# Routing weights of the expert layers spread by DMA from DRAM instead of by TensorE

## The chip, the cores and the metric

The program runs on one core of a Trainium2 chip. The metric is the time of one execution on the device in microseconds (us), the median of several.

## The reference

Tokens are 2 x 1024 vectors of 128 elements. Eight blocks follow one another, each a residual x + f(x), mostly of a layer norm: window attention, a Fourier layer, global and local attention, the Fourier layer again, a location attention, a mixture of experts, a relu-attention block with a feed-forward, and the mixture of experts once more with the same weights. The change is in the mixture of experts, which runs twice:

```python
scores = jax.nn.sigmoid(xt @ gate_w.T)
_, idx = lax.top_k(scores + gate_b, 4)                    # of 16 experts
w = jnp.take_along_axis(scores, idx, axis=-1)
w = w / jnp.sum(w, axis=-1, keepdims=True) * 2.5
comb = zeros((T, 16)).at[arange(T)[:, None], idx].add(w)  # 0 where an expert is not chosen
for each expert e:
    y = y + comb[:, e][:, None] * ((silu(xt @ w1[e].T) * (xt @ w3[e].T)) @ w2[e].T)
y = y + (silu(xt @ w1_s.T) * (xt @ w3_s.T)) @ w2_s.T      # shared expert
```

All 16 experts are computed for every token, and comb puts to zero what wasn't chosen. An expert has 64 hidden rows.

## The kernel before

Activations lie with the 128 features on the partitions and the 2048 tokens along the free axis, in four chunks (c) of 512. Experts are taken in eight pairs (j): a pair fills the 128 partitions with 64 hidden rows of each. Everything of weights and constants stays in SBUF; the engines are programmed by hand, each with its own instruction order, and meet by semaphores. `bank(n)` is one of eight PSUM banks of 128x512 fp32. An fp32 matmul makes two records in the profile. All of TensorE's matmuls carry line 1572, that of the helper `mm`.

`moe_layer` stands once for each engine (lines 685, 971, 1387 and 1917), and is called twice, with i = 0 and 1. Its stages:

- **Logits**: 16 matmuls a half on TensorE give 16 scores a token, tokens on partitions. ACT takes the exponential (line 973), and DVE works out the routing weights `cw` in some ten steps (lines 1407 to 1436), each waiting for the one before (`m_d`). Four more steps (1442 to 1448) split `cw` into three bf16 parts, `cparts`, whose sum is the fp32 value.
- **Early loop** (`ahead`, line 1927): while DVE routes, TensorE makes gate and up of the shared expert (a = 0, 1) and of all eight pairs of chunk 0 (a = 2 to 9); ACT takes silu of gate and copies up (lines 981, 982), POOL multiplies the two (line 695) into buffers from which `hidden_of(a)` reads.
- **Spreading**: TensorE transposes `cparts` by 16 bf16 products with the identity into banks 4 to 7, ACT copies these to `comb` (line 986), 96 rows of bf16 with the three parts stacked. For each (c, j) `spread` (line 1955) multiplies `comb` by a 0/1 matrix from the bf16 constants `bsb`: in PSUM each of a pair's 64 rows per expert then holds that expert's weight for the 512 tokens.
- **Pairs** (line 1979): in the order of (c, j) TensorE issues gate and up of the next pair (not for chunk 0, which has them), the spread of the next pair, the shared expert's down product where j = 0, and the down product of this pair, which accumulates in bank 4 + c. ACT takes silu (line 994) when `m_gu` says that the pair's spread, and so all ahead of it, is done. DVE multiplies up by silu (line 1466), and that by the spread weights in PSUM (line 1469; line 1462 for chunk 0), into `moe[:, 2, k % 2]`, of which there are two; `m_h` releases the down product. At j = 1 DVE adds the chunk before to the residual x (line 1105).

Before the layer POOL clears `cparts` and part of `comb` (lines 688, 690). SyncE issues all DMAs; in the expert layers it has nothing to do but to wait for the output chunks, whose stores are the last four.

## Time and profile before

| | us |
|---|---|
| median of 3 runs | 1099.7 (1099.45 to 1100.71) |
| the profiled execution | 1103.62 |
| its span | 1101.6 |
| TensorE (PE) busy in it | 999.0 (91%) |
| VectorE (DVE) busy | 572.7 (52%) |
| ScalarE (ACT) busy | 557.3 (51%) |
| GpSimd (POOL) busy | 154.3 (14%) |
| mean granted clock of TensorE | 0.936 |

The span is the time from the first to the last instruction in the profile; what the execution takes above it lies around the program. PEld is the loading of weights, which overlaps the products; a busy TensorE is not one at its peak. The chain of work that ended last is followed back from the last instruction, at each step to what released it. A row's bracket tells how long the engine had been idle before it, and what ended that.

### The profile page before, as it was taken

What the parts mean: (1) busy time and instruction counts of PE and PEld (TensorE: products, weight loads), DVE (VectorE), ACT (ScalarE), POOL (GpSimd) and SP (SyncE); (2) the same over time, 40 slices, a digit from 0 to 9 for tenths busy, and PEclk for the clock granted to TensorE, in tenths of its full rate; (3) what the DMA queues carried; (4) which work ended last, traced back from release to release, by engine and by line L of the source; (5) the groups of instructions that cost most, each with busy time, mean ns of one, the idle gap of its engine ahead of it and who ended that gap; (6) DMA issues with size and microseconds to landing.
All of it is one profiled execution on the core that took longest, in us unless ns stands there. A gap on an engine that the chain in (4) does not pass through costs nothing.

```text
span 1101.6 us, 22066 instructions
## 1 busy us (share of the span) xinstructions
PE 999.0 (91%) x9528; PEld 460.5 (42%) x9528; DVE 572.7 (52%) x1134; ACT 557.3 (51%) x767; POOL 154.3 (14%) x168
## 2 busy tenths in 40 slices
PE   6578988989999999877989799998999999999998
PEld 3345655343333334665433344433333333353443
DVE  4465672562333446556455554545666665425454
ACT  5114445659999965543655551127454555445111
POOL 3300102022100101111001140000123223104000
PEclk9569999999999999677999889999999999998999
DMA  9653301000000000000000000000000000000000
GB/s 303 161 142 92 88 17 41 0 20 21 2 3 2 2 2 0 4 4 2 1 0 1 0 1 0 1 0 1 1 3 2 2 3 2 0 1 1 10 10 19
DMA packets 8312, 26.49 MB, mean 24 GB/s; under 512 B 3148, under 2 KB 3468, under 8 KB 6668
## 3 DMA queue, kind: packets, MB, share of 16 engines
q1 hardware_dynamic: 8216, 25.09, 8.3%
q8 instruction: 75, 1.23, 0.5%
q14 instruction: 21, 0.17, 0.1%
HBM read 20.56 MB, written 4.29 MB: 23 GB/s over the span
## 4 chain that ended last, share of the span: by engine, by line
PE 77%; DVE 8%; ACT 8%; issue 3%; DMA 2%; POOL 0%; SPq 0%; DVEq 0%; POOLq 0%
PE ps L1572 76%; ACT nrr L778 1%; ACT nrr L776 1%; DMA stf<-aux 1%; DVE masked L1174 1%; DVE mxq L1180 1%; ACT work L1025 1%; DMA stf<-scr_k 1%; DVE work L1134 1%; DVE work L1526 0%; ACT nrr L765 0%; ACT nrr L762 0%; DVE stf L1540 0%; ACT work L1019 0%; ACT stf L986 0%
## 5 line engine op out<-in xcount | busy, mean ns | idle before, releaser
L1572 PE MATMUL ps<-rq,stf 32*64 32x512 f32 (+4 forms) x4096 | 204.9, 456 | 5.0 <-ACT hz L929 1.6
L1572 PE MATMUL ps<-work,vbuf 64*32 64x96 f32 (+8 forms) x3200 | 202.3, 402 | 6.8 <-issue 5.7
L1572 PE MATMUL ps<-hz,wsb 128*128 128x512 f32 (+1 forms) x352 | 161.1, 623 | 4.0 <-ACT nsq L767 3.5
L885 ACT ACTIVATE work<-ps 128x1024 f32<-128x1024 f32 x144 | 139.4, 1023 | 13.2 <-PE ps L1572 8.9
L1572 PEld LDWEIGHTS ps<-rq,stf 32*64 32x64 f32 x4096 | 95.4, 144 | 107.7 <-issue 79.5
L1572 PEld LDWEIGHTS ps<-work,vbuf 128*32 128x32 f32 (+1 forms) x3200 | 72.7, 119 | 122.4 <-issue 70.1
L947 ACT ACTIVATE work<-ps 128x1024 f32<-128x1024 f32 x72 | 73.7, 1025 | 75.6 <-PE ps L1572 75.6
L824 ACT ACTIVATE work<-ps 128x768 f32<-128x768 f32 x64 | 51.5, 812 | 99.4 <-PE ps L1572 99.4
L1572 PEld LDWEIGHTS ps<-hz,wsb 128*128 128x128 f32 (+1 forms) x352 | 62.9, 191 | 87.7 <-issue 71.2
L994 ACT ACTIVATE work<-ps 128x512 f32<-128x512 f32 x48 | 28.7, 597 | 134.5 <-PE ps L1572 134.5
L1572 PE MATMUL ps<-work,wsb 128*128 128x512 f32 (+1 forms) x176 | 92.6, 622 | 2.7 <-DVE work L1469 2.7
L1247 DVE TENSOR_TENSOR work<-work,csb 128x1024 f32<-128x1024 f32 (+1 forms) x40 | 40.7, 1017 | 96.0 <-ACT work L885 95.6
L1572 PE MATMUL ps<-bsb 128*128 128x384 bf16 x192 | 67.3, 352 | 21.7 <-DMA stf<-scr_k 7.2
L1309 DVE TENSOR_SCALAR work<-ps 128x1024 f32<-128x1024 f32 (+3 forms) x72 | 68.5, 953 | 24.2 <-PE ps L1572 24.2
L1466 DVE TENSOR_TENSOR work<-ps,work 128x512 f32<-128x512 f32 x48 | 33.2, 692 | 72.5 <-ACT work L994 70.8
L1180 DVE TENSOR_REDUCE mxq<-ps 128x2 f32<-128x384 f32 x64 | 35.6, 556 | 44.5 <-PE ps L1572 43.4
L753 ACT ACTIVATE nsq<-ps 128x512 f32<-128x512 f32 x40 | 23.9, 597 | 61.3 <-PE ps L1572 61.3
L682 POOL TENSOR_TENSOR work<-work,csb 128x512 f32<-128x512 f32 (+1 forms) x40 | 36.4, 910 | 106.7 <-ACT work L947 106.7
L1572 PEld LDWEIGHTS ps<-work,wsb 128*128 128x128 f32 (+1 forms) x176 | 31.9, 193 | 44.6 <-issue 20.9
L1572 PE MATMUL ps<-nsq,csb 128*128 128x512 f32 (+3 forms) x152 | 45.0, 516 | 5.1 <-DVE nrr L1263 1.9
L663 POOL TENSOR_SCALAR aux<-nsq,csb 128x1024 f32<-128x1024 f32 x8 | 22.8, 2844 | 159.0 <-DVE nsq L1234 109.2
L1572 PE MATMUL ps<-stf 88*128 88x192 bf16 (+1 forms) x256 | 44.3, 277 | 0.4
(203 smaller groups left out, 1292.1 us busy)
## 6 DMA issues: line engine op xcount, KB each, us to landing
wsb<-in_w SPq DMA_DIRECT2D x1, 3440.0 KB, 19.9
stf<-scr_k SPq DMA_DIRECT2D x12, 204.0 KB
stf<-scr_q SPq DMA_DIRECT2D x12, 192.0 KB
csb<-in_c SPq DMA_DIRECT2D x1, 2099.0 KB, 9.8
rq<-in_rq SPq DMA_DIRECT2D x2, 1024.0 KB, 5.2
scr_q<-work SPq DMA_DIRECT2D x6, 256.0 KB, 6.6
scr_k<-work SPq DMA_DIRECT2D x6, 256.0 KB, 6.3
rq<-scr_k SPq DMA_DIRECT2D x6, 204.0 KB
```

The lines of the kernel that those rows point to most:

```text
L663: nc.gpsimd.tensor_scalar(nums[:, b * S:(b + 1) * S], half_out[0][:, b * S:(b + 1) * S], c_("part")[:, 0:1], None, ALU.mult).then_inc(q["s ...
L682: nc.gpsimd.tensor_tensor(cells, cells, c_("keep").unsqueeze(1).unsqueeze(1) .broadcast_to(list(cells.shape)), ALU.mult).then_inc(q["mk"], 1)
L753: nc.scalar.activation(nsq[:, c], bank(c), ACT.Square).then_inc(n_sq, 1)
L824: nc.scalar.activation(dst, src, ACT.Exp, scale=SCALE).then_inc(q["ex"], 1)
L885: nc.scalar.activation(probs_of(n)[:, 2 * k:2 * k + 2].rearrange("p h s -> p (h s)"), two(slot(2 * n + k)), ACT.Exp, scale=SCALE).then_inc ...
L947: nc.scalar.activation(probs_of(n)[:, 0:2].rearrange("p h s -> p (h s)"), two(slot(2 * n)), ACT.Relu, scale=SCALE).then_inc(q["ex"], 1)
L994: nc.scalar.activation(moe[:, 0, k % 2], bank(k % 2), ACT.Silu).then_inc(m_sg, 1)
L1180: nc.vector.tensor_reduce(mxq[:, k % 2, 2 * u:2 * u + 2], bank(4 + m % 2)[:, 0:2 * W_A].rearrange("p (t s) -> p t s", t=2), AX.X, ALU.max) ...
L1247: nc.vector.tensor_tensor(cells, cells, c_("keep").unsqueeze(1).unsqueeze(1) .broadcast_to(list(cells.shape)), ALU.mult).then_inc(q["mk"], 1)
L1309: ins = nc.vector.tensor_scalar(to[:, :, lo:hi], src[:, :, lo:hi], SCALE, 0.0, ALU.mult, ALU.max)
L1466: nc.vector.tensor_tensor(moe[:, 1, k % 2], bank(2 + k % 2), moe[:, 0, k % 2], ALU.mult)\
L1572: return nc.tensor.matmul(o, l, r, start=start, stop=stop, skip_group_check=True)
```

## The change

The routing weights stay fp32. TensorE transposes `cw` itself (`route_rows`, 16 fp32 transposes, one group of four after each of the early products a = 5 to 8, the first behind a wait for `cw`), ACT copies the 16 rows to `cwt` in SBUF between its early operations, and SyncE stores each chunk of 16x512 to a DRAM tensor `scr_w`. From there SyncE loads for each (c, j) two transfers, one for each expert: 64 partitions, each with the same row of 512 fp32. They go to a ring of eight buffers, `share`, in SBUF; the load of pair k waits till pair k - 8 has been multiplied (`m_h`). DVE's second multiply reads the share from SBUF instead of the spread weights from PSUM, after a wait for the two DMAs (`m_w`). Removed are the spreads, the splitting into three parts, POOL's two memsets, and the matrix of 1024 columns in the bf16 constants. `m_gu` is raised by the up product, `ROUTE_STEPS` is 12.

```diff
+SHARES = 8
-BCOLS = [("ident", 128), ("band_q", 2 * W_A), ("band_a", 2 * W_A),
-         ("spread", NPAIR * 128)]
+BCOLS = [("ident", 128), ("band_q", 2 * W_A), ("band_a", 2 * W_A)]
...
-        comb = stf[:, 0:T // 2].bitcast(BF16)
+        cwt = stf[0:NE, 0:T]
+        share = stf[:, 2 * T:2 * T + SHARES * CH].rearrange("p (k s) -> p k s", k=SHARES)
...
+        scr_w = nc.dram_tensor("scr_w", (NE, T), F32, kind="Internal").ap()
...
+            def shares(i):
+
+                def store(c):
+                    sp.wait_ge(m_cs, NC * i + c + 1)
+                    sp.dma_start(scr_w[:, c * CH:(c + 1) * CH], cwt[:, c * CH:(c + 1) * CH]).then_inc(m_st[c], 16)
+
+                def load(c, j):
+                    k = (i * NC + c) * NPAIR + j
+                    if k >= SHARES:
+                        sp.wait_ge(m_h, k - SHARES + 1)
+                    for e in range(2):
+                        sp.dma_start(share[HB * e:HB * (e + 1), k % SHARES],
+                                     scr_w[2 * j + e, c * CH:(c + 1) * CH].unsqueeze(0).broadcast_to([HB, CH]))\
+                            .then_inc(m_w[k % SHARES], 16)
+
+                store(0)
+                sp.wait_ge(m_st[0], 16 * (i + 1))
+                for j in range(NPAIR):
+                    load(0, j)
+                for c in range(1, NC):
+                    store(c)
+                for c in range(1, NC):
+                    sp.wait_ge(m_st[c], 16 * (i + 1))
+                    for j in range(NPAIR):
+                        load(c, j)
...
             rope_load(1)
+            shares(0)
+            shares(1)
             for c in range(NC):
                 sp.wait_ge(s_res, 4 * U_M1 + c + 1)
...
-                nc.gpsimd.memset(cparts, 0.0).then_inc(m_z, 1)
-                nc.gpsimd.memset(comb[96:P, :], 0.0).then_inc(m_z, 1)
...
+                def rows(c):
+                    act.wait_ge(m_t, NC * i + c + 1)
+                    nc.scalar.activation(cwt[:, c * CH:(c + 1) * CH], bank(4 + c)[0:NE], ACT.Copy).then_inc(m_cs, 1)
...
                     nc.scalar.activation(moe[:, 4, a % 2], bank(2 + a % 2), ACT.Copy).then_inc(e_a, 1)
-                for c in range(NC):
-                    act.wait_ge(m_t, NC * i + c + 1)
-                    nc.scalar.activation(comb[0:96, c * CH:(c + 1) * CH], bank(4 + c)[0:96], ACT.Copy)\
-                        .then_inc(m_cs, 1)
+                    if ROUTED < a <= ROUTED + NC:
+                        rows(a - ROUTED - 1)
...
-                done(nc.vector.tensor_copy(cparts[:, :, 0, 0:NE], cw))
-                done(nc.vector.tensor_tensor(rest, cw, cparts[:, :, 0, 0:NE], ALU.subtract))
-                done(nc.vector.tensor_copy(cparts[:, :, 1, 0:NE], rest))
-                done(nc.vector.tensor_tensor(cparts[:, :, 2, 0:NE], rest, cparts[:, :, 1, 0:NE], ALU.subtract))
...
                         if c == 0:
                             dve.wait_ge(e_m, AHEAD * i + 3 + j)
-                            dve.wait_ge(m_gu, k + 1)
-                            nc.vector.tensor_tensor(moe[:, 2, k % 2], bank(spread_bank(c, j)), hidden_of(2 + j),
+                            dve.wait_ge(m_w[k % SHARES], 32 * (k // SHARES + 1))
+                            nc.vector.tensor_tensor(moe[:, 2, k % 2], hidden_of(2 + j), share[:, k % SHARES],
                                                     ALU.mult).then_inc(m_h, 1)
                             continue
...
                         dve.wait_ge(m_su, full(i, c, j) + 1)
-                        nc.vector.tensor_tensor(moe[:, 2, k % 2], bank(spread_bank(c, j)), moe[:, 1, k % 2],
+                        dve.wait_ge(m_w[k % SHARES], 32 * (k // SHARES + 1))
+                        nc.vector.tensor_tensor(moe[:, 2, k % 2], moe[:, 1, k % 2], share[:, k % SHARES],
                                                 ALU.mult).then_inc(m_h, 1)
...
-                    mm(bank(2 + k % 2), w_("w_up")[:, j * P:(j + 1) * P], ch(z, c))
-                def spread(c, j):
-                    mm(bank(spread_bank(c, j)), b_("spread")[:, j * P:(j + 1) * P], ch(comb, c)).then_inc(m_gu, 1)
+                    mm(bank(2 + k % 2), w_("w_up")[:, j * P:(j + 1) * P], ch(z, c)).then_inc(m_gu, 1)
+                def route_rows(c):
+                    pe.wait_ge(m_d, ROUTE_STEPS * (i + 1))
+                    for tt in range(4):
+                        ins = nc.tensor.transpose(bank(4 + c)[0:NE, tt * P:(tt + 1) * P],
+                                                  rt[:, (4 * c + tt) * NE:(4 * c + tt + 1) * NE], c_("ident"))
+                    ins.then_inc(m_t, 1)
...
                 for a in range(AHEAD):
                     ahead(a)
-                pe.wait_ge(m_d, ROUTE_STEPS * (i + 1))
-                for c in range(NC):
-                    for tt in range(4):
-                        ins = mm(bank(4 + c)[0:96, tt * P:(tt + 1) * P],
-                                 cparts[:, 4 * c + tt].rearrange("p i e -> p (i e)"), b_("ident"))
-                    ins.then_inc(m_t, 1)
-                pe.wait_ge(m_cs, NC * (i + 1))
-                spread(0, 0)
+                    if ROUTED <= a < ROUTED + NC:
+                        route_rows(a - ROUTED)
                 todo = [(c, j) for c in range(NC) for j in range(NPAIR)]
                 for n_, (c, j) in enumerate(todo):
                     if n_ + 1 < len(todo):
                         if todo[n_ + 1][0]:
                             gate_up(*todo[n_ + 1])
-                        spread(*todo[n_ + 1])
                     if j == 0:
+                        pe.wait_ge(m_cs, NC * i + c + 1)
                         shared_down(c)
```

## Rows read from the trace of the kernel before

**Rows 1.** The page, shares of the chain that ended last, by engine

```profile
PE 77%; DVE 8%; ACT 8%; issue 3%; DMA 2%; POOL 0%; SPq 0%; DVEq 0%; POOLq 0%
```

**Rows 2.** Timeline, pair of chunk 1, layer one (start us, length us, engine, line)

```profile
684.67 1.02 PE L1572 MATMUL ps<-work,wsb 128*128 128x512 f32 x2
...
684.87 0.60 ACT L994 ACTIVATE work<-ps 128x512 f32<-128x512 f32 x1 [2.19 <-PE ps L1572]
...
685.53 1.88 PE L1572 MATMUL ps<-hz,wsb 128*128 128x512 f32 x4
...
686.30 0.69 DVE L1469 TENSOR_TENSOR work<-ps,work 128x512 f32<-128x512 f32 x1
...
687.46 1.02 PE L1572 MATMUL ps<-work,wsb 128*128 128x512 f32 x2
```

**Rows 3.** Timeline, from the early loop to chunk 1, first layer

```profile
646.43 0.67 DVE L1436 SCALAR_TENSOR_TENSOR stf<-stf 128x256 f32<-128x256 f32 x1
...
648.95 0.19 PEld L1572 LDWEIGHTS ps<-hz,wsb 128*128 128x128 f32 x1 [0.29 <-ACT work L982]
...
656.20 1.06 PE L1572 MATMUL ps<-bsb,stf 128*96 128x128 bf16 x16
...
659.48 0.60 PE L1572 MATMUL ps<-stf,bsb 128*128 128x512 bf16 x2 [2.22 <-ACT stf L986]
...
670.33 1.88 PE L1572 MATMUL ps<-hz,wsb 128*128 128x512 f32 x4
```

**Rows 4.** Stretches, handover of both layers (engines busy, granted clock, DMA share, GB/s)

```profile
656.20:670.33 14.13, 11.91 (x42) 4.80 (x41) 5.31 (x8) 3.02 (x6) 2.18 (x2) 0.88 0.00 0
...
1010.96:1025.08 14.12, 11.90 (x41) 4.80 (x40) 5.31 (x8) 3.02 (x6) 2.17 (x2) 0.88 0.01 1
```

**Rows 5.** Timeline, last pair of the first layer

```profile
741.86 0.69 DVE L1469 TENSOR_TENSOR work<-ps,work 128x512 f32<-128x512 f32 x1
...
742.60 1.13 PE L1572 MATMUL ps<-work,wsb 128*128 128x512 f32 x2 [1.35 <-DVE work L1469]
```

**Rows 6.** Timeline, an addition with two operands in SBUF

```profile
973.37 0.69 DVE L1114 TENSOR_TENSOR x<-x,hz 128x512 f32<-128x512 f32 x1
```

**Rows 7.** Timeline, transposes ahead of the location attention

```profile
542.61 0.60 PE L2035 MATMUL ps<-csb,hz 128*128 128x128 f32 x4
...
543.04 1.02 PE L1572 MATMUL ps<-hz,wsb 128*128 128x512 f32 x2
```

**Rows 8.** Timeline, start of chunk 1 of the first layer

```profile
674.83 0.38 PE L1572 MATMUL ps<-stf,bsb 128*128 128x512 bf16 x1
...
678.87 0.38 PE L1572 MATMUL ps<-stf,bsb 128*128 128x512 bf16 x1
```

**Rows 9.** DMA issues (KB, median us to landing); issue durations ns, min/median/max

```profile
csb<-in_c SPq DMA_DIRECT2D x1, 128.0 KB, 2.1
...
out_x<-x SPq DMA_DIRECT2D x4, 256.0 KB, 2.0
...
L532 SPq DMA_DIRECT2D stf<-scr_q x12: 651/692/793, 32.1 to 103.8; - x12
...
L538 SPq DMA_DIRECT2D stf<-scr_k x12: 314/366/551, 38.2 to 105.7; - x12
```

**Rows 10.** Timeline, DVE and POOL side by side during the first layer's early loop

```profile
645.23 0.43 DVE L1429 TENSOR_TENSOR stf<-stf 128x256 f32<-128x256 f32 x1
...
648.98 1.30 POOL L695 TENSOR_TENSOR aux<-work 128x512 f32<-128x512 f32 x1 [0.43 <-ACT work L982]
...
649.19 1.37 DVE L1448 TENSOR_TENSOR stf<-stf 128x256 bf16<-128x256 f32 x1
```

**Rows 11.** Stretches, two with loads from the DRAM scratch tensors

```profile
38.20:47.00 8.80, 1.65 (x8) 1.35 (x7) 1.08 (x5) 0.00 (x0) 0.06 (x1) 0.50 0.56 95
...
83.00:95.00 12.00, 8.96 (x86) 5.95 (x85) 5.37 (x26) 3.96 (x5) 0.65 (x2) 0.86 0.52 118
```

**Rows 12.** DMA issues, the bf16 constants

```profile
bsb<-in_b SPq DMA_DIRECT2D x1, 480.0 KB, 5.4
```

More of the change, by code:

```diff
@@ L271, in build @@
         m_t = sem("route_transposed")
-        m_z = sem("route_room_zeroed")
-        m_cs = sem("route_stack")
+        m_st = [sem(f"route_stored{c}") for c in range(NC)]
+        m_w = [sem(f"share_loaded{n}") for n in range(SHARES)]
+        m_cs = sem("route_rows")
         s_ws = sem("shared_down_weights_copied")
@@ L432, in build @@
         AHEAD = 2 + NPAIR
-        ROUTE_STEPS = 16
+        ROUTE_STEPS = 12
+        ROUTED = 5
         SETS = [
@@ L990, in moe_layer @@
                         k = (i * NC + c) * NPAIR + j
-                        act.wait_ge(m_gu, k + 1)
+                        act.wait_ge(m_gu, full(i, c, j) + 1)
                         if full(i, c, j) >= 2:
@@ L1434, in moe_layer @@
                 after()
-                dve.wait_ge(m_z, 2 * (i + 1))
                 done(nc.vector.scalar_tensor_tensor(out=cw, in0=w8, scalar=ROUTE,
@@ L1438, in moe_layer @@
                                                     op0=ALU.mult, op1=ALU.mult))
-                rest = s_
-                after()
-                done(nc.vector.tensor_copy(cparts[:, :, 0, 0:NE], cw))
-                after()
-                done(nc.vector.tensor_tensor(rest, cw, cparts[:, :, 0, 0:NE], ALU.subtract))
-                after()
-                done(nc.vector.tensor_copy(cparts[:, :, 1, 0:NE], rest))
-                after()
-                done(nc.vector.tensor_tensor(cparts[:, :, 2, 0:NE], rest, cparts[:, :, 1, 0:NE], ALU.subtract))
                 assert step[0] == k0 + ROUTE_STEPS
@@ L2165, in bfloat_constants @@
     put("band_a", np.tile(np.where(ok, 0.0, NEG), (1, 2)))
-    spread = np.zeros((P, NPAIR, 2, INTER), np.float32)
-    for e in range(NE):
-        for part in range(3):
-            spread[32 * part + e, e // 2, e % 2, :] = 1.0
-    put("spread", spread.reshape(P, -1))
     return c.astype(BF16_NP)
```

9 lines of the change are left out of this document (removed).

## The prediction

> **What bounds the kernel now.** I read the chain that ended last first: TensorE holds 77% of it, so what leaves TensorE's queue in a stretch where nothing else is late leaves the time too [rows 1]. Then I read the timelines of the two expert layers, because the change touches nothing else but one load at the start. Each layer has three stretches.
>
> In the main one (chunks 1 to 3, 24 expert pairs) the order on TensorE is gate and up of the next pair (four records of 0.43 us), spread of the next pair, down of this one (two records). One pair takes 2.79 us from down to down (684.67 to 687.46). The two records of a down take 0.86, until gate and up start at 685.53 [rows 2]. Six fp32 records at 0.43 fill 2.58, the spread the 0.21 that are left: TensorE is full. Beside it runs a chain of latency: silu starts 0.20 us after the spread has streamed (684.67 to 684.87), then come 0.60 of ACT and two DVE multiplies, the last of which ends at 686.99 [rows 2], in time for the down at 687.46, but not by much.
>
> The stretch ahead of it is the handover: when the last early gate and up product is done TensorE transposes the routing parts (from 656.20), waits 2.22 us for the four ACT copies, starts spreading at 659.48, and reaches gate and up of chunk 1 at 670.33 [rows 3]. That is 14.1 us, and the same stretch of the second layer takes 14.1 us too (1010.96 to 1025.08) [rows 4]. Of useful work only one shared product and seven down products lie in it. The granted clock over it is 0.88 in both layers [rows 4]: TensorE sits idle inside it, and part of it then runs at 1.2 GHz in place of 2.4. In the new order it has no such gap, so I cost chunk 0 at 2.4 GHz.
>
> The third stretch is the early loop: gate and up for two shared and eight routed pairs, four records or 1.72 us each. Its routing weights are ready early: cw starts at 646.43 and takes 0.67, so it is there at 647.10, while the weights of the seventh early pair (a = 6) load at 648.95 [rows 3].
>
> **The change, part by part.**
>
> *Spreads removed, chunks 1 to 3.* 24 a layer at 0.215 us (2.79 less six records of 0.43 [rows 2]): 5.2 us a layer. The signal to ACT moves from the spread to the up product, so the latency chain starts 0.21 earlier too. Counted from the end of the up product it will be as long as it is now from the end of the spread, 684.67 to 686.99 = 2.32 us. Then 0.05 to the weight load (742.55 to 742.60 at the layer's last pair [rows 5]) and at most 0.19 for that load [rows 3]: 2.56. TensorE meanwhile has a down and a gate and up = 2.58. Margin 0.02 us, or more where the load is quicker. DVE gets a further wait (for the share) ahead of its second multiply, and behind it on DVE are only the next pair's multiplies and the chunk's residual; I take it at nothing and bound it by the margin being overrun by 0.05 us a pair, 1.2 us a layer (below nothing it can't go: TensorE has no less to do). The multiply itself now reads two SBUF operands: 0.69 us, as the residual's SBUF add of the same shape shows [rows 6], against 0.69 from PSUM [rows 2]. No gain and no loss there.
>
> *Handover.* New order: after early pair 5, and again after 6, 7 and 8, four fp32 transposes of 128x16. The 128-column transposes of the location attention stand four in 0.43 us (542.61 to 543.04) [rows 7]; 16 cost 1.72 us a layer. They need the routing weights at 648.95 and find them 1.85 us old, so the new wait of TensorE there ends at once. The four copies go between ACT's early work: 1.19 + 0.60 us of ACT beside 2.15 of TensorE, hidden. The early loop ends at 656.20 + 1.72 = 657.9. The shared product of chunk 0 comes at once; such a product adds 4.04 - 2.79 = 1.25 us where it stands in chunk 1 (674.83 to 678.87) [rows 8]. So down of pair 0 may start at 659.2.
>
> Its share must be there: the copy of row block 0 follows early pair 6 (its products end at about 651.5, ACT adds 0.2 + 1.1 + 0.6), 653.4. Store issued at 653.5. A 256 KB store of 2 KB rows lands 2.0 us after its issue, a 128 KB load from DRAM 2.1 [rows 9]. Store landed 655.5, loads from 655.6, the second load of the pair 0.45 later, landed 658.1. Multiply and latency 0.95: 659.1. So the round trip through DRAM is just hidden. After it pairs come at the slowest of three rates: TensorE 0.86, the double-buffered hidden tile 0.96 (from the end of one down: 0.2 to DVE, 0.69, 0.05 and some 0.1 back, 0.86 of the down after next, for two pairs), and the loads. SyncE takes 0.37 us to issue a plain load and 0.69 for one whose source repeats rows [rows 9]; a pair has two, so 0.75 to 1.4 us. I take 1.0, nearest to the plain ones, since this source has only two dimensions. Seven pairs then bring gate and up of chunk 1 to 665.9, against 670.33: 4.4 us. At 0.86 a pair it would be 5.1, at 1.4 a pair 2.1.
>
> *A lock between DVE and POOL.* Two DVE operations on 128x256 with two SBUF inputs take 0.43 and 1.37 us; the long one started at 649.19 beside a POOL product that ran from 648.98 to 650.28, and ended 0.28 after it [rows 10]. The spread multiplies read PSUM; the new ones read two SBUF operands, and POOL's last early product (which shifts with the loop to about 659.4 to 660.7) lies just beside the first ones. At worst one multiply waits 1.3 us for it. I take off half, 0.6 us a layer. The Trainium skill (SBUF — State Buffer, SBUF: two separate sides) says the same in general: DVE with two SBUF inputs and a POOL operation that reads SBUF exclude each other for a whole instruction. By that rule every one of the 32 multiplies is of the kind that can be blocked; by the trace only those beside POOL's last product would be.
>
> *DMA volume.* 64 loads of 128 KB a layer. The final store lands 256 KB of 2 KB rows in 2.0 us with all its fixed parts [rows 9]: a load is at most 1.0 us of the DMA engines, 64 us a layer of some 85, and less as they overlap. Each load is issued up to eight pairs (20 us) ahead. The Trainium skill (SBUF — State Buffer, Door 1) speaks against this shape: 64 partitions reach only eight of the sixteen ports, some 196 GB/s, and two transfers to the two halves serialize. By that, as an estimate, a load takes 0.65 us, a pair 1.3; the handover would gain some 2.5 us in place of 4.4, and the main stretch would gain as much as before; that is within the first rival below. No row here shows 64 partitions loaded alone.
>
> *Nothing for:* POOL's two memsets, DVE's four splitting steps (the last, the long one above, ended at 650.56, TensorE took them up at 656.20 [rows 3, 10]), the stores of chunks 1 to 3 (SyncE issues them behind the first 16 loads, at about 663, lands them at 665; chunk 1 needs its first share at about 669), the output stores queued behind the last loads. If the issue of the first 16 loads took 1.4 a pair, this cover goes and chunk 1 waits about 1 us.
>
> *Start.* The bf16 constants lose 1024 columns, 256 KB of 480 [rows 12]. Other loads share the engines then, and the first stretch also waits on POOL and ACT, so it may bring nothing; at most it brings what 256 KB cost beyond the fixed part, about half of the 2.0 us above [rows 9]. Between 0 and 1 us; I take 0.5.
>
> **Sum.** (5.2 + 4.4 - 0.6) x 2 + 0.5 = 18.5 us. The profiled execution took 1103.62 with a span of 1101.6; it would take 1085.1. The median of the runs, 1099.7, lies 3.9 lower, and the same saving gives 1081.2; I say 1081.
>
> **The rivals.**
>
> *Loads set the pace of chunk 0.* At 0.69 an issue, 6.3 us a layer remain (2.1 - 1.0 + 5.2): 1087. If the loads run as the attention's did, 118 GB/s over 83 to 95 us [rows 11], one takes 1.1 us and a pair 2.2: the first 16 are down at 655.6 + 17.6 + 1.6 = 675, only then is the store of chunk 1 behind them known to be down, its first share lands at about 678.5, and its first down product starts at 679.4, 3.2 us later than before (676.2: the spread at 674.83 [rows 8], its 0.21 and the shared product). The main stretch makes good 4.9 of that: 1.7 us a layer gained, 1096. For it: those loads, the nearest from DRAM scratch with repeated rows, were slow. Against: they move 8 KB rows into 24 partitions, not 2 KB into 64. Chance 0.2, of it 0.04 no more than even.
>
> *All loads read one row.* Each reads the same 2 KB of DRAM 64 times. If that holds each transfer to 1.38 us (128 KB at 95 GB/s, the slowest stretch, 38.2 to 47.0 [rows 11]), 64 of them take 88.3 us from 655.6, and with 2.5 for the last multiply and product the layer ends at 746.4 against 743.7 now (742.60 and 1.13 [rows 5]): 2.7 us a layer, and with the start 1105. The change turns slower from about 1.34 us a load on. For it: nothing in the trace reads one row 64 times, and no row excludes it. The Trainium skill (DMA: Bandwidth & Descriptors, Measured) asks for 1 MiB a transfer; its fixed 2 us would set the pace only if transfers didn't overlap. Chance 0.13.
>
> *The latency chain takes TensorE's place.* If the margin of 0.02 us is really 0.2 below zero (the added wait on DVE costs time, or a weight load can't start while the last gate and up record streams), the main stretch stays at 2.79 a pair and only the handover gains: 1099.7 - 7.6 - 0.5, 1091.5. Chance 0.05.
>
> **How the numbers follow.** Forecast 0.62, its own range 1078 (0.86 a pair, no lock, 1 us at the start) to 1086. Adding the rivals until hardly 2 in 10 are out, and 1 us below for what I may have costed too high: 1077 to 1096. A measurement of this kernel tells 0.2%, 2.2 us, from no change. Faster 0.62 + 0.16 + 0.05 = 0.83; same 0.04; slower 0.13.
>
> **What would show it.** Right: records of down and gate and up 2.58 us apart a pair in the main stretch; gate and up of chunk 1 some 8 us after the last early product; TensorE's clock 1.00 in chunk 0; DVE waiting for nothing but ACT. Wrong: DVE's second multiply released by a DMA of the shares; issues of the shares over 0.7 us each; share loads landing over 4 us after issue; a pair at 2.7 or more with DVE ahead of the down weights.

## The result, and the profile after

The changed kernel takes 1090.16 us (median of 4 runs, 1088.91 to 1091.59), the kernel before, run beside it, 1100.2 (1099.45 to 1103.63). The medians lie 10.0 us apart; the ratio of the runs is 0.9917 (95% interval 0.9892 to 0.9942), which of 1100.2 us is 9.1 us, between 6.4 and 11.9. The forecast was 18.5 us less. The sign and the range were right, the size was not: about half came.

The profiled execution took 1088.91 us with a span of 1085.6, 16.0 less than the span before. About 6 of these 16 lie in parts that both kernels share; from run to run they shift by as much. So I read the layers themselves, from the exponential of the logits to the last down product's start. Layer one: 105.60 before, 100.77 after; layer two: 105.82 and 100.70. That is 4.83 + 5.12 = 9.95 us, and it agrees with the medians. The first window product after the start comes at 46.34 in place of 47.07.

The page of the kernel after: the chain's shares by engine [rows 1], TensorE's busy time, and the new loads among the DMA issues (KB each, us to landing):

```profile
PE 74%; DVE 9%; ACT 8%; DMA 4%; issue 3%; SPq 1%; POOL 0%; DVEq 0%; POOLq 0%
...
PE 986.0 (91%) x9464; PEld 455.1 (42%) x9464; DVE 568.1 (52%) x1126; ACT 557.1 (51%) x767; POOL 147.7 (14%) x164
...
stf<-scr_w SPq DMA_DIRECT2D x128, 128.0 KB, 4.0
```

DMA's share of the chain has doubled, and a share takes 4.0 us to land. Where it enters shows in the timeline of the kernel after, layer one, from the early loop to chunk 1 (start us, length us, engine, line, operation; in brackets the idle time before and what ended it) [rows 3]:

```profile
648.25 0.57 ACT L999 ACTIVATE stf<-ps 16x512 f32<-16x512 f32 x1
...
648.84 0.33 SPq L511 DMA_DIRECT2D scr_w<-stf  x1
...
650.42 10.08 SPq L518 DMA_DIRECT2D stf<-scr_w  x16
...
653.64 2.22 PE L1584 MATMUL ps<-work,wsb 64*128 64x512 f32 x4
...
653.99 0.69 DVE L1473 TENSOR_TENSOR work<-aux,stf 128x512 f32<-128x512 f32 x1 [11.31 <-DMA stf<-scr_w]
...
655.83 0.89 DVE L1473 TENSOR_TENSOR work<-aux,stf 128x512 f32<-128x512 f32 x1 [1.15 <-DMA stf<-scr_w]
656.77 0.30 PEld L1584 LDWEIGHTS ps<-work,wsb 128*128 128x128 f32 x2 [1.74 <-DVE work L1473]
656.77 1.13 PE L1584 MATMUL ps<-work,wsb 128*128 128x512 f32 x2 [0.91 <-DVE work L1473]
657.63 0.69 DVE L1473 TENSOR_TENSOR work<-aux,stf 128x512 f32<-128x512 f32 x1 [0.91 <-DMA stf<-scr_w]
...
660.55 1.51 SPq L511 DMA_DIRECT2D scr_w<-stf  x3
...
664.80 0.69 DVE L1473 TENSOR_TENSOR work<-vbuf,stf 128x512 f32<-128x512 f32 x1 [0.77 <-DMA stf<-scr_w]
...
666.25 0.69 DVE L1473 TENSOR_TENSOR work<-vbuf,stf 128x512 f32<-128x512 f32 x1 [0.75 <-DMA stf<-scr_w]
...
666.51 1.88 PE L1584 MATMUL ps<-hz,wsb 128*128 128x512 f32 x4
```

The store leaves 0.02 us after ACT's copy, the loads 1.58 after that, and the first share is there when the shared product is. From then on DVE waits for a DMA and TensorE for DVE: seven multiplies after the first in 12.26 us (653.99 to 666.25), 1.75 a pair. The same stretch in both layers of the kernel after (engines busy, granted clock, DMA share, GB/s) [rows 4]:

```profile
653.64:666.51 12.87, 8.81 (x18) 2.57 (x17) 5.31 (x8) 1.54 (x3) 1.64 (x2) 1.00 0.94 145
1001.72:1014.23 12.51, 8.84 (x17) 2.57 (x17) 5.34 (x8) 1.54 (x3) 1.64 (x2) 1.00 0.92 152
```

The DMA engines are busy 0.92 to 0.94 of it and move only 145 to 152 GB/s. SyncE isn't the one that is late: it issues the 16 loads of chunk 0 in 10.08 us, 0.63 each or 1.26 a pair, but over these 16 the time from issue to landing grows, from 2.8 us to 6.2: the loads queue up behind their issues. The issues of the shares (ns, min/median/max, first and last start) and their landing in the kernel after, first all of them, then the 16 of chunk 0, layer one:

```profile
L518 SPq DMA_DIRECT2D stf<-scr_w x128: 444/596/1211, 650.4 to 1059.9; - x128
...
DMA to landing us min/median/max: 2.7/4.0/6.2
...
L518 SPq DMA_DIRECT2D stf<-scr_w x16: 496/597/597, 650.4 to 659.9; - x16
...
DMA to landing us min/median/max: 2.8/5.0/6.2
```

The main stretch of the kernel after, where a pair took 2.79 [rows 2]:

```profile
677.20 1.02 PE L1584 MATMUL ps<-work,wsb 128*128 128x512 f32 x2
678.06 1.88 PE L1584 MATMUL ps<-hz,wsb 128*128 128x512 f32 x4
...
679.78 1.02 PE L1584 MATMUL ps<-work,wsb 128*128 128x512 f32 x2
```

Down to down is 2.58 us: TensorE streams without a gap. From gate and up of chunk 1 to the last down product it takes 67.06 and 67.07 us in the two layers, where it took 72.27 and 72.24.

### The profile page after: what moved, and what is told of

It is laid out like the page before. It is cut to its first block, busy times and chain, and to the rows that moved or that the text cites. A ratio compares the mean times of both kernels' runs of the same rounds, so it can differ in the third digit from the quotient of the medians.

```text
span 1085.6 us, 22121 instructions
## 1 busy us (share of the span) xinstructions
PE 986.0 (91%) x9464; PEld 455.1 (42%) x9464; DVE 568.1 (52%) x1126; ACT 557.1 (51%) x767; POOL 147.7 (14%) x164
## 4 chain that ended last, share of the span: by engine, by line
PE 74%; DVE 9%; ACT 8%; DMA 4%; issue 3%; SPq 1%; POOL 0%; DVEq 0%; POOLq 0%
PE ps L1584 73%; DMA stf<-scr_w 1%; ACT nrr L799 1%; ACT nrr L797 1%; DMA stf<-aux 1%; SPq L518 1%; DVE mxq L1202 1%; DVE masked L1196 1%; ACT work L1047 1%; DMA stf<-scr_k 1%; DVE work L1156 1%; DVE work L1538 1%; ACT work L1041 0%; DMA x<-in_x 0%; ACT nrr L786 0%
## 5 line engine op out<-in xcount | busy, mean ns | idle before, releaser
L1584 PE MATMUL ps<-rq,stf 32*64 32x512 f32 (+4 forms) x4096 | 209.9, 466 | 3.0 <-ACT hz L950 1.6
L1584 PEld LDWEIGHTS ps<-rq,stf 32*64 32x64 f32 x4096 | 99.3, 150 | 107.0 <-issue 85.0
```

The source lines that it names most:

```text
L1584: return nc.tensor.matmul(o, l, r, start=start, stop=stop, skip_group_check=True)
```

## The experiments

In all of them two times of a layer are read from the timeline: the handover, from the shared product of chunk 0 to gate and up of chunk 1, and the main stretch, as just given. "Rate" is GB/s and the busy share of the DMA engines over 8 us, from 2 us after the first load of a layer. Totals of single runs scatter by 4 us and more (the kernel before gave 1094 to 1106), so these stretches decide, and totals are given with an interval only where there are several. Each pair of numbers is layer one and two. A whole layer is a coarser measure: its early loop, from the exponential to the shared product, took 20.84 us at a granted clock of 0.92 in layer one of the changed kernel, and 19.20 at 1.00 in that of e4, with the same instructions.

| kernel | different rows a load | handover | main | GB/s at share |
|---|---|---|---|---|
| before | - | 10.31, 10.31 | 72.27, 72.24 | - |
| after | 1 | 12.87, 12.51 | 67.06, 67.07 | 141 at 0.91, 156 at 0.96 |
| e3, chunk 0 loaded early | 1 | 7.91, 7.92 | 67.07, 67.06 | - |
| e1 | 64 | 10.07, 10.07 | 67.07, 67.06 | 204 at 0.70, 203 at 0.75 |
| e10 | 64 | 9.48, 9.45 | 67.06 | 205 at 0.69, 209 at 0.69 |
| e2, 128 partitions | 1 | 13.35, 13.43 | 67.06, 67.18 | 146 at 1.00, 158 at 0.91 |
| e9 | 1 | 12.49, 11.93 | 67.06 | 165 at 0.93, 164 at 0.74 |
| e11 | 1 | 13.01, 12.58 | 67.06, 67.07 | 148 at 0.88, 153 at 0.89 |
| e4, 128 partitions | 2 | 13.17, 12.24 | 67.06 | 147 at 0.83, 167 at 1.00 |
| e6 | 2 | 12.73, 13.10 | 67.06 | 155 at 0.87, 153 at 0.80 |
| e5 | 4 | 13.85, 12.76 | 67.06 | 164 at 0.88, 170 at 0.83 |
| e7, 128 partitions | 8 | 13.70, 13.42 | 67.06 | 167 at 0.96, 172 at 0.82 |
| e14 | 16 | 11.89, 11.51 | 67.06, 67.07 | 170 at 0.89, 172 at 0.75 |
| e8, e7 sooner | 8 | 12.46, 11.84 | 67.06 | 167 at 0.99, 167 at 0.70 |
| e12, e4 sooner | 2 | 11.85, 11.11 | 67.07 | 147 at 0.77, 152 at 0.97 |
| e13, four DMA engines | 16 | 20.80, 21.17 | 68.41, 68.42 | 93 at 0.24, 87 at 0.26 |
| e15, four DMA engines | 4 | 22.32, 21.90 | 68.46, 68.50 | 94 at 0.25, 98 at 0.26 |
| e16, 128 partitions | 128 | 10.70, 10.15 | 67.07, 67.06 | 210 at 0.83, 208 at 0.84 |

**Are the loads what the handover waits for?** e3 takes the supply of chunk 0 off its path: its shares are loaded when the logits are there, before the routing weights, each from one row of in_x.

```diff
-                store(0)
-                sp.wait_ge(m_st[0], 16 * (i + 1))
+                sp.wait_ge(m_log, i + 1)
                 for j in range(NPAIR):
                     load(0, j)
+                store(0)
...
-                                     scr_w[2 * j + e, c * CH:(c + 1) * CH].unsqueeze(0).broadcast_to([HB, CH]))\
+                                     (scr_w if c else xt)[2 * j + e, c * CH:(c + 1) * CH].unsqueeze(0).broadcast_to([HB, CH]))\
```

> The changed kernel, but the 16 loads of chunk 0 are issued some 20 us earlier, as soon as the logits are done, from rows of the input x, so that they wait for no routing weights and no store; everything else stays. It leaves out the right weights for chunk 0. If the loads of chunk 0 (their late start and their rate) are the whole reason why the handover gained nothing, it falls from 21.2 to 16.3 to 17 us, the 0.96 us a pair that the double-buffered hidden tile allows, and the layer gains some 4.5 us. If the exclusion between DVE and POOL or the latency from down product to multiply holds chunk 0, it stays above 19 us.

Measured: 7.91 and 7.92 us. Timeline of e3, TensorE, from the last early pair to chunk 1:

```profile
652.13 1.88 PE L1584 MATMUL ps<-hz,wsb 128*128 128x512 f32 x4
653.94 8.08 PE L1584 MATMUL ps<-work,wsb 64*128 64x512 f32 x16
661.85 1.88 PE L1584 MATMUL ps<-hz,wsb 128*128 128x512 f32 x4
```

With the shares at hand, TensorE's order, DVE's multiplies and the two hidden buffers allow 7.9 us, which is the forecast's 8.0; less the shared product's 1.25 it is 0.95 a pair, near the 0.96 forecast for the hidden buffers. The other 4.6 to 5.0 us of the changed kernel come from the supply of shares. From the exponential to gate and up of chunk 1 e3 takes 28.75 and 28.71 us, the changed kernel 33.71 and 33.63. The one run of e3 took 1080.71 us.

**Is it the rows that repeat?** e1 loads 64 different rows of in_x, as large and to the same places.

```diff
-                                     scr_w[2 * j + e, c * CH:(c + 1) * CH].unsqueeze(0).broadcast_to([HB, CH]))\
+                                     xt[HB * e:HB * (e + 1), c * CH:(c + 1) * CH])\
```

> The changed kernel, but each load of a share takes 64 different rows of 2 KB (of the input x in DRAM) in place of 64 times the same row; number, size and destination of the loads are unchanged. It leaves out the spreading of the routing weights: the hidden rows are multiplied by values of x. What is read: the handover of the first layer, from the start of early product a = 6 to the start of gate and up of chunk 1, which takes 21.2 us in the changed kernel, and the GB/s while the first 16 loads run (145 at a DMA share of 0.94). If reading one row again and again holds the loads back, the rate rises towards 300 and the handover falls to about 18 us (issue at 1.26 us a pair). If the destination of 64 partitions or the packets of 2 KB hold them, both stay (145 to 170 GB/s, 21 us). If the issue of the DMAs holds them, the handover stays too, but the DMA share falls below 0.9.

Measured: 10.07 in both layers (1079.20 us in its one run). Stretch of e1, layer one, and below it the 16 loads of chunk 0 and their landing:

```profile
650.40:658.40 8.00, 6.83 (x14) 2.00 (x13) 3.91 (x5) 2.21 (x5) 2.53 (x2) 1.00 0.70 204
...
L518 SPq DMA_DIRECT2D stf<-in_x x16: 535/596/597, 648.4 to 657.9; - x16
...
DMA to landing us min/median/max: 3.0/3.2/3.4
```

More bytes in less busy time: 204 GB/s at 0.70, where the changed kernel has 141 at 0.91. The handover falls by 2.4 to 2.8 us, a little over half of the gap to e3. The loads no longer queue up: each lands 3.0 to 3.4 us after its issue, the last like the first (3.0 to 3.3 in layer two), where in the changed kernel the time grew to 6.2. So the transfers keep up with SyncE, and what sets e1's pace is the issue, 16 loads in 10.12 us, 1.26 a pair.

**Is it the half width, or two issues a pair?** e2 has one load for each pair, of one row to all 128 partitions.

```diff
-                    for e in range(2):
-                        sp.dma_start(share[HB * e:HB * (e + 1), k % SHARES],
-                                     scr_w[2 * j + e, c * CH:(c + 1) * CH].unsqueeze(0).broadcast_to([HB, CH]))\
-                            .then_inc(m_w[k % SHARES], 16)
+                    sp.dma_start(share[:, k % SHARES],
+                                 scr_w[2 * j, c * CH:(c + 1) * CH].unsqueeze(0).broadcast_to([P, CH]))\
+                        .then_inc(m_w[k % SHARES], 16)
```

> The changed kernel, but one load for each pair brings one row of 2 KB to all 128 partitions: the same bytes, the same single source row for each DMA, half as many DMAs. It leaves out the weights of the odd experts, whose hidden rows get those of the even one. If the destination of 64 partitions holds the loads back, the rate roughly doubles (about 300 GB/s), the DMA share falls and the handover goes from 21.2 to about 17 us. If the source row does, the rate stays at 145 to 170 GB/s and the handover at 21. If the issue of the DMAs does (0.63 us each), the handover falls to about 17 us while the rate per busy engine stays as it is, near 10 GB/s.

Measured: 13.35 and 13.43, with 146 GB/s in layer one:

```profile
654.10:662.10 8.00, 6.52 (x12) 1.79 (x10) 2.25 (x4) 2.28 (x5) 2.81 (x2) 0.82 1.00 146
```

With the engines at 1.00 neither the width nor the issues matter: the first eight loads are issued in 7.1 and 6.8 us instead of sixteen in 10.1, and DVE gets its shares no sooner. e4 does the same with each expert's own weights: hidden rows of a pair's two experts take turns on the partitions (host code reorders w1, w3 and w2 to match), and one load reads the two rows in turn.

```diff
+                    sp.dma_start(share[:, k % SHARES],
+                                 scr_w[2 * j:2 * j + 2, c * CH:(c + 1) * CH].unsqueeze(0).broadcast_to([HB, 2, CH]))\
+                        .then_inc(m_w[k % SHARES], 16)
...
+    def turns(a):
+        return a.reshape(P, NPAIR, 2, INTER).transpose(0, 1, 3, 2).reshape(P, -1)
```

> The changed kernel with the hidden rows of the two experts of a pair interleaved (the host packs gate, up and down weights so that partition 2r + e holds row r of expert e), so that one load a pair fills all 128 partitions: its source repeats 64 times the two rows of the pair, 64 outermost. It computes everything. Same bytes, half the DMAs. If 64 partitions as destination hold the loads back: handover about 17 us, two layers 8 us less than the changed kernel, 1082. If the repeated source row does: no change, 1090. If the issue does: a pair needs one issue of 0.6 to 0.7 us, handover 17 us as in the first case, but at about 10 GB/s a busy engine.

Measured: 1089.41 us, ratio 0.9918 (0.9887 to 0.9948), the changed kernel's own; handover 13.17 and 12.24.

**Is it where the row lies, or that it was just written?** e9 reads one row of the input tensor, e10 64 different rows of an old scratch tensor of the program (scr_q), e11 keeps the routing weights in rows of the output tensor.

```diff
e9
+                                     xt[2 * j + e, c * CH:(c + 1) * CH].unsqueeze(0).broadcast_to([HB, CH]))\
e10
+                        to = stf[HB * e:HB * (e + 1), 2 * T + (k % SHARES) * CH:2 * T + (k % SHARES + 1) * CH]
+                        sp.dma_start(to.bitcast(BF16), scr_q[c % B, j % 3].rearrange("g d h s -> (g d h) s")[HB * e:HB * (e + 1), :])\
e11
-        scr_w = nc.dram_tensor("scr_w", (NE, T), F32, kind="Internal").ap()
+        scr_w = out[0:NE, :]
```

> The changed kernel, but each load of a share repeats 64 times one row of the input x in DRAM, in place of one row of the scratch tensor; everything else stays, the store and the wait for it too. It leaves out the right routing weights. The run with 64 different rows of the same tensor had 205 GB/s at a DMA share of 0.72 (17.8 GB/s for each busy engine) and a handover of 10.1 us; the changed kernel has 144 GB/s at 1.00 (9) and 12.9. Theory A, the repeated row: as the changed kernel. Theory B, the scratch tensor (its place, or that it was written a moment ago): as the run with different rows, 10.1 us a handover, 98 us a layer, 1079. In between (15 GB/s a busy engine, as the early loads of one row of x had) if both play a part; the handover is then 10.1 to 11.

> The changed kernel, but each load takes 64 different rows of 2 KB from the scratch tensor of the window attention's queries, which the program wrote 600 us earlier. It leaves out the routing weights (the bits of other data stand for them). Theory B1, a scratch tensor of the program is slower to read than an input tensor, whenever it was written: 9 to 11 GB/s a busy engine, DMA share near 1.0, handover 12.5 to 13.5 us. Theory B2, what was written a moment ago is slow to read: here it is old, so 17 to 18 GB/s, share 0.72, handover 10.1. Theory A (repeats) expects 10.1 too, and the run with one row of x tells it apart.

> The changed kernel, but the routing weights are stored in rows 0 to 15 of the output tensor, chunk by chunk at the place of their own chunk, which gets its final values only after all of its shares were used; one row is repeated 64 times by each load as in the changed kernel. It computes everything. Theory B1 (place of the tensor): handover 10.1 to 11 us and 98 a layer, 5 to 6 us less than the changed kernel in all. Theories A and B2 (repeats; freshly written): 12.5 to 13 us and 100.8, no change.

Measured: e9 12.49 and 11.93, e10 9.48 and 9.45, e11 13.01 and 12.58 (1091.41 us, ratio 0.9918, 0.9887 to 0.9949). Stretch of e9, layer one:

```profile
649.40:657.40 8.00, 6.08 (x13) 1.71 (x12) 2.77 (x4) 2.25 (x5) 2.52 (x2) 1.00 0.93 165
```

and of e10, layer one:

```profile
654.40:662.40 8.00, 7.04 (x16) 2.10 (x14) 4.78 (x6) 2.27 (x5) 2.53 (x2) 1.00 0.69 205
```

Scratch memory with different rows is as quick as the input with different rows, and the input with one row nearly as slow as scratch with one. The repeated row is the main cause, not the tensor nor its fresh writing. The input's one row keeps a small lead, 165 against 141 and 156 and a handover 0.4 to 0.6 us shorter, that I can't explain; so a small part for the tensor or its fresh writing isn't excluded.

**How many copies would do?** e6 and e5 store each row two and four times, and a load reads the copies in turn; e7 is e5 with e4's single load.

```diff
+        COPIES_W = 4
+        scr_w = nc.dram_tensor("scr_w", (NE, COPIES_W, T), F32, kind="Internal").ap()
...
+                    sp.dma_start(scr_w[:, :, c * CH:(c + 1) * CH], cwt[:, c * CH:(c + 1) * CH].unsqueeze(1)
+                                 .broadcast_to([NE, COPIES_W, CH])).then_inc(m_st[c], 16)
...
+                                     scr_w[2 * j + e, :, c * CH:(c + 1) * CH].unsqueeze(0)
+                                     .broadcast_to([HB // COPIES_W, COPIES_W, CH]))\
```

> As the run with four copies, but with two, so that each row is read 32 times in a load. Theory A: between the changed kernel (144 GB/s, handover 12.9 and 12.5 us) and the one with four copies; if what counts is how many reads of one row come close together, the rate is near the full one already, and if the limit were a fixed rate for each row it would double to above what the issue of the loads allows (205 GB/s), so that two copies do as well as four. Theory B: no change, 144 GB/s.

> The changed kernel, but the store puts each row of routing weights four times into DRAM, 8 KB apart, and each load repeats these four rows 16 times in place of one row 64 times. It computes everything. Theory A, repeated reading of one DRAM row holds the loads back: with a quarter of the repeats the rate during the 16 loads of chunk 0 goes from 144 GB/s at a DMA share of 1.00 to near the 201 to 205 GB/s of the run with 64 different rows, the handover (shared product of chunk 0 to gate and up of chunk 1) from 12.9 and 12.5 us to 10.1 to 10.8, and the layer (exponential of the logits to its last down product) from 100.8 to 98 to 99: about 1085. Theory B, what made the run with different rows faster was something else (a tensor in another place of the DRAM, or that it was not freshly written): no change, 100.8 a layer, 1090.

> Four copies of each row as above, and one load of 128 partitions for a pair (the hidden rows of its two experts lie in turns of four, packed by the host), so half as many DMAs. It computes everything. With one row for each expert this halving gained nothing (handover 13.2 and 12.2 us). If the repeated row was the first limit and the issue of two loads a pair (1.26 us) the second, both are gone now: over 250 GB/s while the loads run, handover 8.5 to 9.5 us, a layer 96.5 to 97.5, 1082. If the destination of 64 partitions or the issue never mattered, it does as the run with four copies and two loads a pair (10.1 to 10.8 us).

Measured: the rate rises a little, to 153 to 155 and then 164 to 172 GB/s, and the handover does not fall (12.7 to 13.9). Four copies make the first store slower: e5 issues it at 650.15 and can load from 653.16, 3.0 us later, where the changed kernel needs 1.58. That eats what the rate brings. e6 gave 1089.23 us in its one run. e5 gave 1089.39 us, ratio 0.9871 (0.9806 to 0.9936), over runs of 1080.88 to 1096.76; e7 1094.26, ratio 0.9925 (0.9893 to 0.9957).

**Starting sooner.** e8 is e7, and e12 is e4 with e11's place, each with the transposes one early pair sooner.

```diff
-        ROUTED = 5
+        ROUTED = 4
```

> As the run before, and TensorE transposes the routing weights one early product sooner (after a = 4 to 7 in place of 5 to 8), so that the first store leaves 1.7 us earlier. It computes everything. If what is then left of the handover above the 7.9 us of the run with early loads is the late first share, it falls to 7.9 to 8.2 us, a layer to 96, 1080; TensorE's wait for the routing weights stays under 0.2 us, as they are 1.85 us old at a = 5. If the weights come too late for a = 4, TensorE stalls there by some tenths of a us, and DVE's routing steps, which POOL delays, decide.

> The run before with one load of 128 partitions a pair (hidden rows of two experts in turns) and the transposes one early product sooner. It computes everything. Under B1 the transfer no longer holds chunk 0, the halved issue (0.6 us a pair) and the store that leaves 1.7 us earlier come through: handover 7.9 to 8.8 us, 96 a layer, 10 us less than the changed kernel. Under A or B2: handover about 12, the 1.7 us of the earlier store and no more.

Measured: e8 12.46 and 11.84, 1087.11 us, ratio 0.9844 (0.9800 to 0.9888); e12 11.85 and 11.11, 1085.49 us, ratio 0.9872 (0.9826 to 0.9918). The handovers are 1.1 to 1.6 us shorter than those of e7 and e4. Whole layers, from the exponential to the last down product, take 100.43 and 100.56 us in e8 and 99.83 and 98.81 in e12, against 100.77 and 100.70 in the changed kernel: e8 gains 0.5 us on it in all, e12 2.8, of which 2.4 lie in the two handovers. Their medians lie 3.1 and 4.7 below its 1090.16. The ratio of e12 overlaps that of the changed kernel (0.9892 to 0.9942); that of e8 ends just below it, at 0.9888, although its layers gain only 0.5 us. That either is quicker than the changed kernel is likely by the handovers (1.1 and 2.4 us less in all), but small beside the scatter of the totals, and which of the two is the quicker isn't settled.

**Number of readings, or engines that read one row at once?** In e13 and e14 a load has 16 different rows of in_x; e15 is e5 in the other order.

```diff
e13
+                                     xt[16 * e:16 * (e + 1), c * CH:(c + 1) * CH].unsqueeze(0).broadcast_to([4, 16, CH]))\
e14
+                                     xt[16 * e:16 * (e + 1), c * CH:(c + 1) * CH].unsqueeze(1).broadcast_to([16, 4, CH]))\
e15
+                                     scr_w[2 * j + e, :, c * CH:(c + 1) * CH].unsqueeze(1)
+                                     .broadcast_to([COPIES_W, HB // COPIES_W, CH]))\
```

> Loads as in the change, but each of 64 partitions takes its row from 16 different rows of in_x, 8 KB apart, partition p from row p mod 16; the spreading of weights is left out. Each row is read 4 times a load, by rows that lie 16 partitions apart. If the rate falls with how often a row is read in one load, 4 readings come near the 205 GB/s of 64 different rows: handover 10.1 to 10.7 us. If it falls because several DMA engines read the same row at the same time, it stays at 145 to 170 GB/s with a DMA share of 0.85 to 1.0, handover 12 to 13.5. Main stretch 67.07 either way.

> The same 16 rows of in_x, but partition p takes row p / 4, so that the four readings of one row follow one another; the spreading of weights is left out. If the rate goes by the number of readings alone, it equals the run with p mod 16. If it goes by engines that read the same row at once, this one is the faster of the two: about 200 GB/s at a DMA share of 0.7, handover about 10.1, against 12 to 13.5. If readings one behind the other are the slow ones, it is the slower of the two.

> The changed kernel with each row stored four times, as with the four copies before, but 16 neighbouring partitions read the same copy (p / 16 in place of p mod 4). If engines that read the same row at once are what slows the loads, fewer do so here: 180 GB/s or more and a handover of 11.5 to 12.2 instead of 13.85 and 12.76. If only the number of readings counts, 165 to 170 GB/s and a handover of 12.8 to 13.9 as before.

Measured: e13 handover 20.80 and 21.17, e15 22.32 and 21.90 (1106.88 us in its one run, 1104.27 for the kernel before beside it: the gain is gone), e14 11.89 and 11.51. Neither reading had foreseen that. Stretch of e13, layer one:

```profile
650.60:658.60 8.00, 4.38 (x8) 1.30 (x8) 1.96 (x2) 2.24 (x5) 2.52 (x2) 0.94 0.24 93
```

and of e14:

```profile
653.50:661.50 8.00, 6.13 (x13) 1.74 (x12) 2.82 (x4) 2.29 (x5) 2.52 (x2) 1.00 0.89 170
```

A share of 0.24 (e15: 0.25 and 0.26) is four engines of sixteen: these two sources have 4 as their outermost count, all others 16 or more. The Trainium skill (DMA: Bandwidth & Descriptors, Rules for kernel authors) says so: a slowest dimension of less than 16 confines the transfer to as many engines. The runs agree. So e13 and e14 can't be set against each other, but each says something. In e13 and e15 four engines move 87 to 98 GB/s, 22 to 25 each, although in e15, if each of the four takes one of the four outermost counts, an engine reads the same row 16 times, and in e13 16 different ones: an engine alone isn't slow at reading a row again. In e14 each engine has, if the outermost count is dealt out evenly, one row of its own, and it is no quicker than e5, where four rows serve all (170 and 172 against 164 and 170). That speaks against engines that read one row at once as the cause, but doesn't exclude it. What falls is the total that sixteen engines reach together: 203 to 209 GB/s with 64 different rows, 170 to 172 with 16, 167 to 172 with 8, 164 to 170 with 4, 147 to 167 with 2, 141 to 165 with 1. The step from 64 rows to 16 is clear, below 16 the values overlap. Which part of the way to DRAM makes it so no run shows.

**Is the rest SyncE's issuing?** e16 loads 128 different rows by one transfer a pair.

```diff
+                    sp.dma_start(share[:, k % SHARES], xt[:, c * CH:(c + 1) * CH])\
+                        .then_inc(m_w[k % SHARES], 16)
```

> One load a pair of 128 different rows of in_x to 128 partitions; the spreading of weights is left out. It has half the issues of the run with 64 different rows a load, whose rate was what SyncE could issue (128 KB each 0.63 us, 205 GB/s at a DMA share of 0.7). If the issues were its limit, the rate rises to 260 GB/s or more at a share of 0.9 or more, and the handover falls from 10.07 to 8.6 to 9.5. If the destination or another part of the path is the limit at about 205 GB/s, both stay: 10.0 to 10.3.

Measured: 10.70 and 10.15, and in layer one

```profile
652.10:660.10 8.00, 6.37 (x14) 1.81 (x12) 4.14 (x5) 2.29 (x5) 2.53 (x2) 1.00 0.83 210
```

The eight loads of chunk 0 and their landing, layer one:

```profile
L517 SPq DMA_DIRECT2D stf<-in_x x8: 347/432/1299, 650.1 to 654.5; - x8
...
DMA to landing us min/median/max: 3.5/7.0/9.0
```

SyncE issues the eight loads in 5.6 us, in little more than half of the time of e1's sixteen, and the rate stays at 208 to 210. Now the loads queue up, from 3.5 us to 9.0 between issue and landing: the transfers set the pace, 1.25 us a pair (256 KB at 210 GB/s). In e1 they didn't, the landing stayed at 3.0 to 3.4, and SyncE's issues set 1.26. Two limits lie side by side, so halving the issues alone brings nothing. What 64-partition loads of different rows would reach with quicker issues no run shows.

## Why the prediction was right or wrong

**Spreads removed: right.** Forecast 5.2 us a layer, measured 5.21 and 5.17. The latency chain with its margin of 0.02 us holds: in all the kernels whose loads reach all engines a main stretch is 67.06 to 67.18. DVE waited for a share once in the two main stretches, 0.4 us in layer two, and that stretch is no longer for it. The multiply with two SBUF operands took 0.69, as [rows 6] had it.

**Handover: wrong, by the pace of the loads.** The first steps came out: transposes 0.43 a group, the copy at once, the shared product at the end of the early loop, the first down product 1.1 us behind it (forecast 1.3). From the store's issue at 648.84 to the first multiply at 653.99, store and load took 5.15 us, forecast 4.6. Then the step that failed, "a pair has two issues, 0.75 to 1.4 us, I take 1.0": it measured 1.75. The issues alone take 1.26 a pair, and repeating or plain makes no difference: the record of one is 0.60 us in the median in the changed kernel and in e1. The transfers of the repeated row take more than that. The forecast asked only what an issue costs and left the transfer itself at "at most 1.0 us" a load, which it used for the layer as a whole and not for the eight pairs that need 2 MB at once. 1.0 us a pair is 262 GB/s; none of the stretches of loads read here came above 210. In place of 8.0 us, and 0.6 for the lock, the handover took 12.87 and 12.51. With the early loop counted in, from the exponential to gate and up of chunk 1, it took 33.33 and 33.58 us before and 33.71 and 33.63 after: 0.4 and 0.05 us lost where 3.8 were to be gained. That is the whole miss: 3.8 x 2 + 0.4 = 8.0, and 18.5 - 8.0 = 10.5, against the 10.0 between the medians. Two of the prediction's signs of being wrong came with it: DVE's second multiply is released by a DMA of the shares, and the share loads of chunk 0 land up to 6.2 us after their issue.

How it divides: from 12.7 (mean of the changed kernel) 2.6 to 3.2 us go with different rows (e1, e10), and a further 1.5 to 2.2 only when the loads come early (e3). The first part is the repeated row. The second is the late start together with SyncE's 1.26 us a pair, which e1 and e10 still have; the runs don't divide it further.

**Lock of DVE and POOL: there, but free.** One multiply a layer is stretched, to 0.89 and 0.93 us, 1.22 in e5. In layer one POOL's last early product ran from 654.91 to 656.17, and the multiply that started beside it ended at 656.72, 0.55 later; the others kept their 0.69. DVE waits for the next share anyway. Where shares came sooner it showed more: in e1 two multiplies took 1.97 us together.

**Clock: right.** 1.00 over the handover, where it was 0.88 [rows 4]: TensorE's pauses of 0.3 to 0.9 us between down products did not lower it, while e2 has 0.82 in the stretch shown and e5 0.79 in the same one.

**Start: not shown.** The first window product came 0.7 us sooner, 0.5 forecast, but in the sixteen other kernels with the same smaller constants it starts anywhere from 45.22 to 47.83 us, before and behind the 47.07 of the kernel before. That it fits is luck.

**Port reach.** The estimate from the Trainium skill (SBUF — State Buffer, Door 1), 1.3 us a pair for loads to 64 partitions (128 KB at its 196 GB/s are 0.67 us, so 1.34), is near what e1 and e10 come to, 1.26. But that is the pace of the issues there, and the loads of chunk 0 landed a steady 3.0 to 3.4 us (e1, layer one) and 2.6 to 2.9 us (e10) after theirs, so neither shows a limit of the ports. With all 128 partitions the rate was no more than 208 to 210 (e16), and with repeated rows the width made no difference (e2).

**The rivals.** The first is what happened: the loads set the pace of chunk 0. It stood at 1087 (issue time) or 1096 (118 GB/s), with chance 0.2, and 1090 lies between. It priced a pair at 1.4 or 2.2 us, and 1.75 was measured; the sum took 1.0. Its doubt, that 8 KB rows into 24 partitions are another case than 2 KB into 64, was a reason to call 118 GB/s low, not to take 262. The second rival had the right mechanism, loads that read one row, at the wrong price: 141 to 156 GB/s are 0.8 to 0.9 us a load, not 1.38, and the 48 loads of chunks 1 to 3 still fit beside their 24 pairs: 1.75 us of loads a pair, 2.58 of TensorE. The third, the latency chain, did not occur.

## What to carry to other kernels

When data go through DRAM on their way to the next stage, price the burst, not the layer: bytes that the first consumers need, divided by the rate that such loads reach, counted from the moment the store is down. A row that is broadcast by DMA here came at 141 to 165 GB/s, where different rows came as fast as SyncE issued them, at 203 to 209. To tell the two limits apart, look at the time from issue to landing over a burst: where it grows, the transfers are late, where it stays, the issues are. Give such loads a start ahead of need (e3 shows 4.8 us a layer for it), keep at least 16 as the outermost count, and do not pay for copies of the row with a slower store.

## What the runs showed of the hardware

- Loads of 2 KB rows, 16 DMA engines busy: 203 to 210 GB/s when all rows of a load differ (64 or 128), 141 to 167 when they are one or two rows, with a mostly higher busy share (0.69 to 0.84 against 0.74 to 1.00). Different rows of an input and of an old scratch tensor came alike (203 to 204, 205 to 209); one row of the input at 164 to 165, of scratch at 141 to 156, of the output tensor at 148 to 153.
- 16 loads of 128 KB issued one behind the other: with different rows each lands 3.0 to 3.4 us after its issue (e1), with one row 2.8 for the first and 6.2 for the last (changed kernel).
- Four engines alone moved 87 to 98 GB/s, 22 to 25 each (e13, e15); sixteen together at most 210 with loads of shares, 13 each (e16).
- A DRAM store of 32 KB and a load that depends on it: 1.58 us from issue to issue, 2.36 with 64 KB (e6), 3.0 with 128 KB (e5).
- SyncE needed 0.63 us for each load of 128 KB one behind the other, whether the source repeats (changed kernel) or not (e1).
- A DVE multiply with two SBUF operands that started while POOL's product ran ended 0.55 us after it (656.17 and 656.72 in the changed kernel, 657.47 and 658.02 in e5) and took 0.89 and 1.22 us in place of 0.69. In e2 the multiply started first and kept its 0.69, and POOL's product took 1.55 us in place of 1.26.
